# Layernorm phase of a recurrent + MoE kernel: a second buffer for the input tiles, and the statistics of a tile moved ahead of the normalising of the one before

## What is computed

```python
xn = _layernorm(x, axis=-1)                      # x: 2 x 8192 tokens, D = 1024
u  = einsum('btd,ds->bts', xn, B)                # recurrent layer, 64 states
hs = scan over t of  h = sigmoid(A_diag) * h + u_t
s  = hs @ C + xn @ D
f  = xn + mlp(xn, shared) + sum over the top 2 of 16 experts of w_e * mlp(xn, e)
x  = x + s * silu(f)                             # mlp(x) = (silu(x@wg) * (x@wu)) @ wd, I = 512
```

## Time and profile before

| | |
|---|---|
| median of 2 runs | 1838.44 us (1836.53 to 1840.36) |
| the profiled execution's own time | 1837.29 us |
| its span on the slowest core (core 4) | 1835.4 us |
| spans of the 8 cores | 1826.9 to 1835.4 us |
| mean granted TensorE clock | 0.951 to 0.955 of full speed |
| busy: PE / DVE / ACT / POOL | 86% / 52% / 11% / 2% |

### The profile page before, as it was taken

How to read it: one execution, slowest core, us unless ns; L and a number is a source line. 1 busy time by engine, 2 the same in 40 slices (tenths; PEclk the granted TensorE clock), 3 DMA queues, 4 the chain that set the end, 5 groups by cost and what they waited for, 6 DMA issues and landing times.

```text
span 1835.4 us, 18621 instructions; the slowest of 8 cores (1826.9 to 1835.4 us)
## 1 busy us (share of the span) xinstructions
PE 1584.1 (86%) x7074; PEld 683.6 (37%) x7074; DVE 958.2 (52%) x1982; ACT 200.4 (11%) x355; POOL 28.0 (2%) x32
## 2 busy tenths in 40 slices
PE   0134255799999999999999999999999999999987
PEld 0000022344444444444444444444444444444432
DVE  0267743545565555555555655555655545564532
ACT  0000011111111111111111111111111111111111
POOL 1000000000000000000000000000000000000012
PEclk9975577899999999999999999999999999999999
DMA  8921110112121312121221213221212212121058
GB/s 154 151 94 46 46 46 1 46 46 92 46 92 56 126 49 92 47 92 62 76 92 47 92 47 112 72 93 47 92 46 92 92 46 92 47 94 44 9 107 115
DMA packets 58873, 134.78 MB, mean 73 GB/s; under 512 B 3793, under 2 KB 8018, under 8 KB 57762
## 3 DMA queue, kind: packets, MB, share of 16 engines
q1 hardware_dynamic: 48354, 120.66, 19.9%
q0 software_dynamic: 10432, 12.95, 5.2%
HBM read 129.76 MB, written 16.78 MB: 80 GB/s over the span
## 4 chain that ended last, share of the span: by engine, by line
PE 81%; DVE 7%; another core or an unknown queue 4%; DMA 4%; issue 1%; ACT 1%; DVEq 1%; POOLq 0%; ACTq 0%; SPq 0%
PE pb L58 81%; DMA out<-inter_sb 3%; DVE acc L58 2%; DVE x L58 1%; DVEq L70 1%; DVE inter_sb L58 1%; DVE xnT L58 1%; DMA xt_buf<-xt 1%; DVE xb L58 0%; DMA xt_buf<-dmat 0%; DVE rD L58 0%; DVE rA L58 0%; ACT L58 0%; DVE warena L58 0%
## 5 line engine op out<-in xcount | busy, mean ns | idle before, releaser
L58 PE MATMUL pb<-xnT,warena 128*128 128x512 bf16 x4608 | 1032.4, 382 | 3.5 <-DVE t_sb L58 3.5
L58 PEld LDWEIGHTS pb<-xnT,warena 128*128 128x128 bf16 x4608 | 445.3, 98 | 553.6 <-issue 38.5
L58 PE MATMUL pb<-inter_sb,warena 128*128 128x512 bf16 x2176 | 491.5, 379 | 2.5 <-DVE acc L58 2.5
L58 DVE TENSOR_TENSOR t_sb<-silu_sb,pb 128x512 bf16<-128x512 bf16 x272 | 186.6, 686 | 552.3 <-ACT silu_sb L58 552.3
L58 DVE TENSOR_TENSOR acc<-acc,pb 128x512 f32<-128x512 f32 x576 | 369.0, 684 | 107.6 <-PE pb L58 107.3
L58 PEld LDWEIGHTS pb<-inter_sb,warena 128*128 128x128 bf16 x2176 | 212.6, 98 | 259.9 <-issue 4.5
L58 ACT ACTIVATE silu_sb<-pb 128x512 bf16<-128x512 f32 x272 | 162.4, 597 | 1240.0 <-PE pb L58 1239.9
L58 DVE CAST warena<-xt_buf 128x512 bf16<-128x512 f32 (+1 forms) x320 | 130.7, 480 | 1.5 <-DMA xt_buf<-dmat 1.5
L58 PE MATMUL pb<-xb,onesc 128*1 128x512 bf16 (+1 forms) x40 | 21.2, 530 | 97.7 <-DVE x L58 97.7
L58 DVE TENSOR_TENSOR inter_sb<-t_sb,m_sb 128x512 bf16<-128x512 bf16 x256 | 91.8, 420 | 5.9
L58 PE MATMUL pb<-xnT,bsb 128*64 128x512 bf16 (+1 forms) x40 | 16.3, 588 | 56.2 <-DVEq L58 56.2
(11 more groups left out here) (68 smaller groups left out, 227.6 us busy)
## 6 DMA issues: line engine op xcount, KB each, us to landing
xt_buf<-ewu SPq DMA_DIRECT2D x16, 2048.0 KB
xt_buf<-ewd SPq DMA_DIRECT2D x16, 2048.0 KB
xt_buf<-ewg SPq DMA_DIRECT2D x15, 2048.0 KB
out<-xt SPq DMA_DIRECT2D x1, 8192.0 KB
xt_buf<-xt SPq DMA_DIRECT2D x8, 1024.0 KB, 7.8
out<-inter_sb POOLq DMA_DIRECT2D x16, 512.0 KB, 7.0
xt_buf<-dmat SPq DMA_DIRECT2D x2, 2048.0 KB
xt_buf<-xt SPq DMA_DIRECT2D x2, 512.0 KB, 66.1
```

Of the source, the lines that this page charges most:

```text
L58: return Inst(getattr(self.real, name)(*a, **kw))
```

## The change

`emit_tile` is cut into three parts. `emit_tile_front(it)` is the load and the statistics, `emit_tile_mid(it)` is from the wait for the last statistics matmul to the Exp, and `emit_tile_back(it)` is the rest, from DVE's wait for the Exp to the scan. They are called in the order front(0), mid(0), front(1), back(0), mid(1), front(2), back(1), mid(2), front(3), back(2), mid(3), front(4), back(3), mid(4), back(4).

- Even tiles are loaded into `xt_buf` as before. Odd tiles are loaded in four quarters of two chunks into the four MLP buffers, read as f32, with two semaphores of their own (`s_xb`, `s_xb2`). The load of tile `it` waits for the last subtraction of tile `it-2`; tiles 0 and 1 wait for nothing.
- Odd tiles sum their statistics, and spread mean and rstd, in banks 0 and 1 instead of 4 and 5.
- Tile 0's normalising, which writes `x2`, waits for the last statistics matmul of tile 1. The first two casts of a tile wait for the matmuls that read `xb` for the tile before.
- `PHASE_A_V` becomes the last subtraction of tile 4.

```diff
-            def emit_tile(it):
+            def xt_v(it, c, w=TB):
+                if it % 2 == 0:
+                    return xt_buf[:, c * TB:c * TB + w]
+                return xt2_f[c // 2][:, (c % 2) * TB:(c % 2) * TB + w]
+
+            def emit_tile_front(it):
...
-                if it > 0:
-                    SY.wait(sv, XT_FREE[it - 1])
+                sb0, sb1 = (4, 5) if it % 2 == 0 else (0, 1)
+                if it >= 2:
+                    SY.wait(sv, XT_FREE[it - 2])
...
+                else:
+                    for q in range(4):
+                        dst = xt2_f[q].rearrange("p (c t) -> p c t", c=2)[:, :, 0:W]
+                        ins = SY.op("dma_start", out=dst,
+                                    in_=xsrc[:, 2 * q:2 * q + 2, off:off + W])
+                        ins.inc(sxb if q < 2 else sxb2, 16)
...
+                    if it >= 1 and c < 2:
+                        V.wait(spe, stats_mm_t[(it - 1, c + 6)])
...
-                k = SC.op("activation", rA[:, 0:W], rB[:, 0:W], AF.Exp,
-                          scale=-0.5).inc(ssc, 1)
-                V.wait(ssc, k)
+                EXP_T[it] = SC.op("activation", rA[:, 0:W], rB[:, 0:W], AF.Exp,
+                                  scale=-0.5).inc(ssc, 1)
+
+            def emit_tile_back(it):
...
+                V.wait(ssc, EXP_T[it])
...
                 if it == 4:
-                    PHASE_A_V = SCAN_T[4]
+                    PHASE_A_V = XT_FREE[4]
...
-            for it in range(5):
-                emit_tile(it)
+            emit_tile_front(0)
+            emit_tile_mid(0)
+            emit_tile_front(1)
+            emit_tile_back(0)
+            emit_tile_mid(1)
+            emit_tile_front(2)
+            emit_tile_back(1)
...
```

More of the change, by code:

```diff
@@ L152, in build_nc @@
         pb = [ps(f"pb{i}", [128, 512]) for i in range(8)]
-        sem_names = ["s_x", "s_x2", "s_o", "s_o1", "s_gc", "s_w0", "s_w1", "s_w2", "s_w3",
+        sem_names = ["s_x", "s_x2", "s_xb", "s_xb2", "s_o", "s_o1", "s_gc",
+                     "s_w0", "s_w1", "s_w2", "s_w3",
                      "s_pe", "s_v", "s_sc", "s_gp"]
@@ L183, in emit @@
             sx, sx2, sgc = S["s_x"], S["s_x2"], S["s_gc"]
+            sxb, sxb2 = S["s_xb"], S["s_xb2"]
             so_sems = [S["s_o"], S["s_o1"]]
@@ L322, in emit @@
             n_sx2 = [0]
+            n_sxb = [0]
+            n_sxb2 = [0]
             prev_gacc = 0
@@ L332, in emit @@
             PHASE_A_V = None
-            def emit_tile(it):
-                nonlocal n_sx, prev_rt_consumed, prev_topk, prev_mevac, PHASE_A_V, prev_gacc
-                off, W = A_TILES[it]
-                own = it >= 1
-                tb = it - 1
-                if it > 0:
-                    SY.wait(sv, XT_FREE[it - 1])
[L341 to L350, removed]
+            EXP_T = {}
@@ new lines, in emit @@
+            xt2_f = [silu_sb[:, :].bitcast(F32), t1_sb[:, :].bitcast(F32),
+                     inter_sb[:, :].bitcast(F32), inter2_sb[:, :].bitcast(F32)]
+            def xt_v(it, c, w=TB):
[3 more added lines that the diff above has]
+            def emit_tile_front(it):
+                nonlocal n_sx
+                off, W = A_TILES[it]
+                sb0, sb1 = (4, 5) if it % 2 == 0 else (0, 1)
+                if it >= 2:
+                    SY.wait(sv, XT_FREE[it - 2])
+                xsrc = xt.rearrange("(c p) t -> p c t", p=128)
+                if it % 2 == 0:
+                    SY.op("dma_start",
+                          out=xt_buf[:, :].rearrange("p (c t) -> p c t", c=8)[:, 0:4, 0:W],
+                          in_=xsrc[:, 0:4, off:off + W]).inc(sx, 16)
+                    n_sx += 1
+                    SY.op("dma_start",
+                          out=xt_buf[:, :].rearrange("p (c t) -> p c t", c=8)[:, 4:8, 0:W],
+                          in_=xsrc[:, 4:8, off:off + W]).inc(sx2, 16)
+                    n_sx2[0] += 1
+                else:
[4 more added lines that the diff above has]
+                        ins.inc(sxb if q < 2 else sxb2, 16)
+                    n_sxb[0] += 2
+                    n_sxb2[0] += 2
+                c0s, c0n = (sx, 16 * n_sx) if it % 2 == 0 else (sxb, 16 * n_sxb[0])
+                c4s, c4n = (sx2, 16 * n_sx2[0]) if it % 2 == 0 else (sxb2, 16 * n_sxb2[0])
@@ L352, in emit_tile @@
                 for c in range(8):
                     if c == 0:
-                        V.wait(sx, 16 * n_sx)
+                        V.wait(c0s, c0n)
                     if c == 4:
-                        V.wait(sx2, 16 * n_sx2[0])
+                        V.wait(c4s, c4n)
+                    if it >= 1 and c < 2:
+                        V.wait(spe, stats_mm_t[(it - 1, c + 6)])
                     if c >= 2:
@@ L359, in emit_tile @@
                     V.op("tensor_copy", xb[:, (c % 2) * TB:(c % 2) * TB + W],
-                         xt_c(c, W))
+                         xt_v(it, c, W))
                     k = V.op("tensor_tensor", x2[:, (c % 4) * TB:(c % 4) * TB + W],
-                             xt_c(c, W), xt_c(c, W), ALU.mult).inc(sv, 1)
+                             xt_v(it, c, W), xt_v(it, c, W), ALU.mult).inc(sv, 1)
                     if c == 0:
@@ L365, in emit_tile @@
                             T.wait(sgc, 16 * n_gc)
-                        T.wait(sx, 16 * n_sx)
-                        t_wait_bank(4)
-                        t_wait_bank(5)
+                        T.wait(c0s, c0n)
+                        t_wait_bank(sb0)
+                        t_wait_bank(sb1)
                     T.wait(sv, k)
-                    T.op("matmul", pb[4][0:1, 0:W], onesc[:, :],
+                    T.op("matmul", pb[sb0][0:1, 0:W], onesc[:, :],
                          xb[:, (c % 2) * TB:(c % 2) * TB + W],
                          start=(c == 0), stop=(c == 7))
-                    kk = T.op("matmul", pb[5][0:1, 0:W], onesc[:, :],
+                    kk = T.op("matmul", pb[sb1][0:1, 0:W], onesc[:, :],
                               x2[:, (c % 4) * TB:(c % 4) * TB + W],
@@ L376, in emit_tile, with emit_tile_mid @@
                     stats_mm_t[(it, c)] = kk
+            def emit_tile_mid(it):
+                off, W = A_TILES[it]
+                sb0, sb1 = (4, 5) if it % 2 == 0 else (0, 1)
                 V.wait(spe, stats_mm_t[(it, 7)])
-                V.op("tensor_copy", rA[:, 0:W], pb[4][0:1, 0:W])
-                k = V.op("tensor_single_scalar", rB[:, 0:W], pb[5][0:1, 0:W],
+                V.op("tensor_copy", rA[:, 0:W], pb[sb0][0:1, 0:W])
+                k = V.op("tensor_single_scalar", rB[:, 0:W], pb[sb1][0:1, 0:W],
                          float(D) * EPS, ALU.add).inc(sv, 1)
-                lastv[4] = lastv[5] = k
+                lastv[sb0] = lastv[sb1] = k
                 V.drain()
@@ L392, in emit_tile @@
                 SC.drain()
-                k = SC.op("activation", rA[:, 0:W], rB[:, 0:W], AF.Exp,
-                          scale=-0.5).inc(ssc, 1)
-                V.wait(ssc, k)
+                EXP_T[it] = SC.op("activation", rA[:, 0:W], rB[:, 0:W], AF.Exp,
+                                  scale=-0.5).inc(ssc, 1)
+            def emit_tile_back(it):
+                nonlocal PHASE_A_V
+                off, W = A_TILES[it]
+                sb0, sb1 = (4, 5) if it % 2 == 0 else (0, 1)
+                own = it >= 1
+                tb = it - 1
+                V.wait(ssc, EXP_T[it])
                 V.op("tensor_copy", rCb[:, 0:W], rC[:, 0:W])
@@ L398, in emit_tile @@
                 T.wait(sv, k)
-                t_wait_bank(4)
-                t_wait_bank(5)
-                T.op("matmul", pb[4][:, 0:W], onesrb[:, :], rCb[:, 0:W],
+                t_wait_bank(sb0)
+                t_wait_bank(sb1)
+                T.op("matmul", pb[sb0][:, 0:W], onesrb[:, :], rCb[:, 0:W],
                      start=True, stop=True)
-                k = T.op("matmul", pb[5][:, 0:W], onesrb[:, :], rAb[:, 0:W],
+                k = T.op("matmul", pb[sb1][:, 0:W], onesrb[:, :], rAb[:, 0:W],
                          start=True, stop=True).inc(spe, 1)
@@ L408, in emit_tile @@
                     for c in range(8):
-                        kk = V.op("tensor_tensor", acc_v(c, tb), xt_c(c),
-                                  pb[4][:, 0:TB], ALU.subtract)
+                        kk = V.op("tensor_tensor", acc_v(c, tb), xt_v(it, c),
+                                  pb[sb0][:, 0:TB], ALU.subtract)
                     XT_FREE[it] = kk.inc(sv, 1)
@@ L414, in emit_tile @@
                         V.op("tensor_tensor", acc_v(c, tb), acc_v(c, tb),
-                             pb[5][:, 0:TB], ALU.mult)
+                             pb[sb1][:, 0:TB], ALU.mult)
                     V.drain()
@@ L420, in emit_tile @@
                 else:
+                    V.wait(spe, stats_mm_t[(1, 7)])
                     for r0 in (0, 4):
@@ L423, in emit_tile @@
                             kk = V.op("tensor_tensor", x2[:, (c - r0) * W:(c - r0 + 1) * W],
```

(18 more changed lines are left out.)

## The result

The changed kernel takes 1823.25 us (median; before 1838.38 in the same series). The ratio is 0.9917 with a 95% interval of 0.9905 to 0.9928, a gain of 15.1 us where 8.8 were forecast. The forecast was 1829.6; the range held the time by 0.25 us at its lower end. Both are well within 2% of the time before.

The account below looks back on a forecast made before the run. Phase A, where DVE and TensorE wait for each other in turn, was taken to move the end one for one. 15.4 us freed less 6.6 given back made 8.8, from 1838.44 to 1829.6 us; range 1823 to 1839.

Parts of the forecast that it names:

- (a): DVE's wait for ScalarE's Ln and Exp: hidden under the next tile's statistics except in tile 4, 5.7 us freed.
- (b): DVE's wait for the last statistics matmul: gone for tiles 1 to 4, tile 0's 0.84 stays, 4.7 us freed.
- (c): DVE's wait for tile 1's load before its first cast: gone through the early load, 5.0 us freed.
- d: DVE's wait for the spreading matmuls, now behind the next tile's statistics on TensorE: longer, 1.3 us given back.
- g: Tile 2's load, with 7.9 us of cover: 1.6 us of new waiting before its statistics, ends 0 and 3.5.
- f: The start: tile 1's early packets take turns with gsb's late rows, 3.3 us given back, ends 0 and 12.3.
- e: TensorE's clock in the statistics: the fast half may be lost after a longer gap, 0.4 us given back.
- the free start: Rival, chance 0.2: early load does not delay gsb; 12.1 us gained, 1826.3 us, or 1824.7 with a shorter tile 2 load.
- The starved start: Rival, chance 0.1: all of tile 1 passes ahead of gsb's last rows, 12.3 us at the start, 1840.5 us.
- The clock's rival: Rival, chance 0.08: the wide tiles' four fronts all run at TensorE's upper clock level; 14.8 us gained, 1823.6 us.
- the gain is not passed on: Rival, chance 0.05: something behind phase A tied to the start takes the gain back, 1838.4 us.

Follow-up runs that it names:

- e3: Changed kernel plus sixteen DVE copies between the next tile's statistics and the casts of mean and rstd, leaving TensorE idle before the spreading pair; 1851.0 us (one run).
- e4: Changed kernel with each tile's scan, and DVE's wait for the multiplication by B, moved behind the next tile's mean and variance; 1809.87 us, ratio 0.9845.
- e1: Changed kernel, but SyncE issues tile 1's load only when GpSimd's eight constants have landed; 1829.6 us, ratio 0.9952.
- e5: Changed kernel with the 8 MB copy of the residual issued behind tile 4's load instead of ahead of tile 0's; 1776.02 us, ratio 0.9647.

## Why the prediction was right, and where it was off

The place, the path and the sign were right. Phase A is on the path one for one, the waits (a) and (b) went to the pieces named (7.2 to 1.5, 5.06 to 0.8 as the mean of the cores), and the early load removed tile 1's wait (c). The sum of 8.8 us was too small by six, mostly from terms of give-back that came smaller or not at all (d 2.4, g 1.5 and f 1.1 us as means of the cores, e 0.4). That the range still held the time is partly luck: its lower end was the free start less 1.9, and the start was not free.

- *d, the spreading matmuls*, is the step whose mechanism failed. The prediction said: "The wait becomes 1.27 + 1.01 - 0.75 = 1.53 instead of 1.26". The 1.01 came from a pair that had followed 5.81 us of idle TensorE; behind the statistics it takes 0.59, and the wait is 0.84. The 1.27 shrank with it: the statistics now end 0.80 us after DVE's last square (118.78 to 119.58), against 1.16 in tile 2 before, since their last two matmuls run fast as well. Tile 0's wait did not grow either (0.77). Over the mean of the cores the waits fell by 1.1 us where 1.3 more were charged, 2.4 us in all. e3 shows the cause by putting the idle time back.
- *g, tile 2's load*, was charged 1.6 and cost nothing on seven of eight cores, 0.7 on one, in the first profile. The 9.5 us taken for it were those of tile 1's load at the end of the weights; behind them a tile's first half took under 7.7 us (7.3 in e4), and e1 shows 15 beside more of them. Nothing was the lower end of the stated range.
- *e, the clock in the statistics*, cost its 0.4 in tile 2 (8.39 to 118.78 - 109.96 = 8.82, on the slowest cores), and tile 4's statistics gained as much (8.81 to 8.41).
- *f, the start*, charged with 3.3, is 2.2 with a standard error of 0.7. (The 77.5 of the slowest core looks like the 78 of the forecast, but one core scatters by 2.7.) That the size came near is luck. The product 39 x 0.085 has all 39 packets one behind another on one DMA engine, since 0.085 us is the time of a packet on one engine. In the packet times of the trace sixteen of the 39 are four-byte writes and most others rows of 32 bytes, and these start in clusters, five of them between 70.10 and 70.16 us, so several engines worked side by side; spread over 16 of them the product would be an estimated 0.2 us. What makes the start later stays open. For the large copy, e5 shows that GpSimd's constants wait for q1's traffic.
- By waits alone phase A lost 5.7 + 4.3 + 1.1 + 4.8 = 15.9 us; it became 16.5 shorter. The rest I put to the overlap of neighbouring DVE instructions, which start some 0.07 us before the one ahead ends where no wait stands between (118.10 + 0.68 = 118.78 against 118.70 above); nine waits went, which would make 0.6. That was not tested.

Of the rivals, the free start came nearest in time (1824.7 us with tile 2's load at its lower end), though the start was not free. The starved start is excluded: gsb came 2 us later, not 12. The clock's rival named the right engine and the wrong place: the fronts ran mostly at the lower level, as before (half of tile 2's at the upper one before, half of tile 4's now), and what gained was the pair behind them and the last matmuls ahead of it. That the gain is not passed on is excluded by the equal lengths behind phase A.

## What to carry to other kernels

A duration that a row shows holds for what the engine did before it. When work is moved, ask what will stand ahead of it in its new place; here the last statistics matmuls run at the upper level, and a pair put right behind them inherits that. The trace of the kernel before gave only a hint of it: the last matmuls ran fast in tile 1 (0.38) but took 0.58 to 0.63 in tiles 2 to 4. And read the longest wait ahead of everything: the reordering of phase A gave 15 us, the plain move of one large copy behind the small loads on another queue gave 47, and both with the scan moved as well 75 (1763.9 us).

## What was not expected of the hardware

Half a tile, 1 MB, took 15 us when it was issued at 77 us in e1, while the weight loads of q0, which cast on the way, had 1.77 MB still to move. In the changed kernel, issued at 102 us with 0.04 MB left on q0, it took under 7.7. The load's own queue was empty ahead of it both times.

How q0 and q1 share the DMA engines depends on what they carry. Beside the large copy their packets come in pairs: in the packet times of the slowest core, 196 of q0's 206 packets from 20 to 30 us are followed, 11 to 14 ns after their start, by the start of a q1 packet of their own (with q0's starts moved by a few tenths of a us, some 50 find one within 20 ns). That shows the turns of one for one that the prediction took from the counts. Beside the weights it is not so clear: in the changed kernel, 68 to 70 us on core 0,

```profile
q0 software_dynamic: 171, 0.15, 52.5%
q1 hardware_dynamic: 159, 0.30, 49.9%
```

the numbers are nearly equal, but the starts are paired no more than by chance, and in e1 from 83 to 89 us q1 had 494 packets to q0's 375. The Trainium skill ("DMA: Bandwidth & Descriptors", "Queues, rings and completion order") has an engine change between queues after a packet of typically 9 to 17 descriptors; the pairs beside the large copy do not agree with turns so long, and the later counts cannot tell.
